# Turning a row of softmax maxima with a VectorE block transpose and eight small transfers per group, where TensorE transposes, a ScalarE eviction and two transfers did it

## The chip, the cores and the metric

The kernel runs on one core of a Trainium2 chip. The metric is the device time of one execution in microseconds (us); lower is better. All times below are in us unless marked ns. The engines are TensorE (PE in the profile, its weight loads PEld), VectorE (DVE), ScalarE (ACT), GpSimd (POOL) and SyncE (SP), which here only issues transfers (DMAs).

## The reference

Two transformer blocks with modulated layer norms act on x of shape (8, 512, 256): attention with 16 heads of width 16, then a feed-forward part. The first block's feed-forward is a gated one with four wide products, the second's is a group of experts. Only attention matters here:

```python
x = L0_attn_x                                    # (8, 512, 256)
h = _layernorm(x) * (1 + ca) + sa
x = x + ga * _L0_attn_ref(h, ...)                # q, k are RMS-normed and rotated
h = _layernorm(x) * (1 + cb) + sb
x = x + gb * _L0_ffn_ref(h, ...)
h = _layernorm(x) * (1 + ca) + sa                # second block, its own ca, sa, ...
x = x + ga * _L1_attn_ref(h, ...)
x = x + gb * _L1_ffn_ref(h, ...)
# inside either attention, for every batch b and head h (T = 512, hd = 16):
scores = jnp.einsum('bhtd,bhsd->bhts', qh, kh) / sqrt(hd)
attn   = softmax(scores, axis=-1)
y      = jnp.einsum('bhts,bhsd->bhtd', attn, vh)
```

## The kernel before

The program is four stages, one after the other: attention of the first block (tiles named A0 in the order below, plain A in the profile; 82 to 600 us of the profiled execution with what precedes its first product), the gated feed-forward (B), attention of the second block (A1 in the order, A in the profile; its first product at 1293.6 us) and the experts (D). The change is in both attention stages.

An attention stage handles 8 batches. The 16 heads of a batch are 4 **groups** of 4 heads; a group is called G and counts from 0 to 31 in a stage. The heads lie in pairs, `a` = 0 and 1, in partitions 0 to 48 and 64 to 112 of the tiles KT (keys) and QS (queries): 48 rows are the high and low parts of 16 features, and row 48 of QS (`QROWS - 1`) holds the negated maximum of each query's scores, so that the product that makes the scores subtracts the maximum as it goes (row 48 of KT is 1).

All engines run one loop over a step p; each writes its own list of instructions for every step, and semaphores alone bind the lists together. In step p:

- TensorE makes two raw products, `SM<-KT,QS` (line 1031; products 2p + 28 and 2p + 29 of the stage, 14 steps ahead of the scores they serve), two score products `ST<-QS,KT` (line 1047), then a **job** if the table has one at p, then `values` (line 1064) in the steps p = 8G + 3, 5, 6, 8. A job is one bank's worth of other work (a projection, transposes); nearly all jobs write the same PSUM bank X, and each waits until the one before it has been evicted.
- VectorE takes the maximum over 512 keys of each raw product, with its sign turned (line 822), 16 for each group, and evicts the jobs P0 and P1 (line 830), both after the step's two maxima.
- ScalarE takes the exponential of 1024 columns of scores (line 584) and evicts most of the other jobs.

SM has two banks, so a raw product waits for the maximum two before it. The maxima of group G are taken in steps 8G - 14 to 8G - 7. They lie as a column for each head and block of 128 queries, one query per partition, and must become a row for each head in QS before step 8G. That is the job MT at step 8G - 5: four transposes of `M` on TensorE into bank X (line 964, a wait for all 16 maxima ahead), an eviction to the tile MT on ScalarE (line 593) at the head of the next step, and at step 8G - 3 on SyncE two transfers of two rows of 1 KB (line 336, columns "A_QS<-A_MT"). TensorE waits for their semaphore `row_ld` before the scores of step 8G.

Other jobs sit at steps that are 1, 2, 4 and 7 mod 8; MT alone is at 3 mod 8, where `values` stand too. In the first block's stage the job before MT is P0 in one group of four (step 18 of each 32) and a projection whose bank ScalarE reads twice (QK, line 610 and `A_sq`, line 613) or once (V) in the others.

SyncE also moves each batch's queries and keys through memory: it loads them back with eight loads of high parts and four of low parts (lines 323 and 329, 128 KB each, called HIGH and LOWS in the tables). Line 1031 waits for all twelve of batch b at step 32b - 14. In the second block's stage the LOWS stand at steps 32b - 21 and 32b - 20, with the store of a finished batch (`y<-A_yT`, line 384) between them.

## Time and profile before

| | us |
|---|---|
| median of 3 runs | 2140.57 |
| lowest and highest of them | 2139.06, 2143.35 |
| the profiled execution, its own time | 2137.07 |
| span of that execution, first to last instruction | 2135.4 |
| TensorE busy | 1860.6 (87%) |
| VectorE busy | 1352.1 (63%) |
| ScalarE busy | 1209.8 (57%) |
| GpSimd busy | 577.1 (27%) |
| attention of the first block, first raw product to last scores | 82.5 to 580.6 |
| attention of the second block, likewise | 1293.6 to 1758.0 |

The span is the time from the first to the last instruction of the profiled execution; 1.7 us of its time lie around it. Busy shares are means over four unlike stages. In a row of the timeline the first number is the start in us from the span's start, the second the duration; what stands in brackets is how long the engine was idle before it and what released it.

### The profile page before, as it was taken

The numbers are of one execution on the slowest core, as the hardware profiler recorded it, in microseconds if no ns is written. First come the engines' busy times: TensorE is split into PE (matmuls) and PEld (weight loads), VectorE is DVE, ScalarE is ACT, GpSimd is POOL, SyncE is SP. The second block draws the span as 40 slices with busy tenths as digits, with TensorE's granted clock in tenths as the row PEclk, the third lists the DMA queues.
The fourth block names the chain that finished last, engine by engine and source line by source line (L and its number), as shares of the span: only waits on it lengthen the run. The fifth ranks groups of instructions, "written<-read, shape, count | busy, mean of one in ns | idle before, by whom it ended". The sixth has DMA issues, their size and how long they took to land. (4 is left out here: it accounts for less than half of the span.)

```text
span 2135.4 us, 29721 instructions
## 1 busy us (share of the span) xinstructions
PE 1860.6 (87%) x10573; PEld 763.6 (36%) x10573; DVE 1352.1 (63%) x2591; ACT 1209.8 (57%) x1686; POOL 577.1 (27%) x668
## 2 busy tenths in 40 slices
PE   5789999988849999999999987899999883888887
PEld 3323332322214444444444442233333221444443
DVE  5578888888624544544534534888888854676771
ACT  4378887776713433333333323888888773565563
POOL 4666667662200000000001022111111001344343
PEclk8689999999979999999999996999999995899999
DMA  3344544334250000000000021233333305323210
GB/s 110 60 107 100 134 121 124 106 106 112 95 217 1 21 21 1 22 21 1 22 18 28 21 50 45 55 69 62 70 61 60 60 11 177 105 101 131 85 40 20
DMA packets 111987, 147.92 MB, mean 69 GB/s; under 512 B 11875, under 2 KB 95189, under 8 KB 109781
## 3 DMA queue, kind: packets, MB, share of 16 engines
q1 hardware_dynamic: 111828, 145.77, 25.6%
q8 instruction: 104, 1.70, 0.4%
q14 instruction: 55, 0.44, 0.1%
HBM read 100.34 MB, written 45.14 MB: 68 GB/s over the span
## 5 line engine op out<-in xcount | busy, mean ns | idle before, releaser
L822 DVE TENSOR_REDUCE A_M<-A_SM 128x1 f16<-128x512 f32 x1024 | 654.4, 687 | 176.4 <-PE A_SM L1031 174.6
L584 ACT ACTIVATE A_P<-A_ST 128x1024 f32<-128x1024 f32 x512 | 523.9, 1026 | 128.6 <-PE A_ST L1047 124.3
L1031 PE MATMUL A_SM<-A_KT,A_QS 48*128 48x512 f16 x1024 | 351.3, 399 | 62.1 <-DVE A_M L822 54.0
L1573 PE MATMUL B_PA<-B_Hh,B_wh 128*128 128x512 f16 x1024 | 388.1, 379 | 0.0
L1573 PE MATMUL B_PA<-B_Hl,B_wh 128*128 128x512 f16 x1024 | 388.1, 379 | 0.0
L1491 ACT ACTIVATE B_af<-B_PA,B_sv 128x512 f32<-128x512 f32 x192 | 132.0, 688 | 367.0 <-PE B_PA L1573 366.9
L1047 PE MATMUL A_ST<-A_QS,A_KT 49*128 49x512 f16 x1024 | 299.9, 386 | 0.3
L1064 PE MATMUL A_AV<-A_P,A_V 128*32 128x512 f32 x2048 | 278.6, 608 | 5.3 <-ACT A_P L584 4.8
L1031 PEld LDWEIGHTS A_SM<-A_KT,A_QS 48*128 48x128 f16 x1024 | 82.4, 93 | 439.5 <-DVE A_M L822 385.2
L1535 DVE TENSOR_SCALAR B_Hh<-B_af 128x512 f16<-128x512 f32 x128 | 58.4, 456 | 281.3 <-ACT B_af L1491 281.3
L1289 POOL TENSOR_TENSOR B_hl<-B_hf,B_hh 128x512 f16<-128x512 f32 x14 | 16.2, 1155 | 543.0 <-ACT B_hh L1305 543.0
L1573 PEld LDWEIGHTS B_PA<-B_Hl,B_wh 128*128 128x128 f16 x1024 | 100.2, 98 | 118.9
L1573 PEld LDWEIGHTS B_PA<-B_Hh,B_wh 128*128 128x128 f16 x1024 | 100.2, 98 | 118.7
L1537 DVE SCALAR_TENSOR_TENSOR B_Hl<-B_af,B_Hh 128x512 f16<-128x512 f32 x128 | 88.6, 693 | 4.4
L1529 DVE SCALAR_TENSOR_TENSOR B_uf<-B_PD,B_sv,B_af 128x512 f32<-128x512 f32 x64 | 47.8, 747 | 54.0 <-PE B_PD L1573 29.6
L550 POOL TENSOR_TENSOR A_tr<-A_qkf,A_tr 128x512 f16<-128x512 f32 x28 | 32.4, 1157 | 156.7 <-ACT A_tr L678 156.7
L1491 ACT ACT_TABLE_LOAD x23 | 29.5, 1283 | 65.6 <-PE B_PA L1573 52.8
L1064 PEld LDWEIGHTS A_AV<-A_P,A_V 128*32 128x32 f32 x2048 | 44.4, 108 | 62.2 <-issue 50.0
L1573 PE MATMUL B_PA<-B_hh,B_wh 128*128 128x512 f16 x128 | 51.0, 399 | 17.0 <-issue 16.9
L934 PE MATMUL A_X<-A_wh,A_hh 128*128 128x256 f16 (+1 forms) x160 | 52.5, 328 | 9.9 <-ACT A_V L628 7.4
L1047 PEld LDWEIGHTS A_ST<-A_QS,A_KT 49*128 49x128 f16 x1024 | 55.5, 94 | 14.4 <-ACT A_P L584 12.3
L2054 DVE SCALAR_TENSOR_TENSOR D_Hl<-D_af,D_Hh 128x512 f16<-128x512 f32 x64 | 45.3, 744 | 16.9 <-ACT D_Hh L1922 16.9
(334 smaller groups left out, 3287.6 us busy)
## 6 DMA issues: line engine op xcount, KB each, us to landing
D_w_st<-in_we_dram SPq DMA_DIRECT2D x16, 1024.0 KB, 4.9
qk<-A_tr SPq DMA_DIRECT2D x58, 256.0 KB, 2.5
A_KT<-qk SPq DMA_DIRECT2D x96, 128.0 KB, 4.7
A_QS<-qk SPq DMA_DIRECT2D x96, 128.0 KB, 5.2
A_w_st<-in_w_ffn_dram SPq DMA_DIRECT2D x32, 352.0 KB, 3.6
w_hi<-A_f_hi SPq DMA_DIRECT2D x32, 176.0 KB, 3.4
w_lo<-A_f_lo SPq DMA_DIRECT2D x32, 176.0 KB, 3.8
B_wl<-w_lo SPq DMA_DIRECT2D x1, 5632.0 KB, 22.5
```

The costliest lines, as they stand in the source:

```text
L584: nc.scalar.activation(P[:, st, 2 * pair:2 * pair + 2, :], ST[:, u % 2, :, :], ACT.Exp, scale=1.0 / math.sqrt(HD)).then_inc(exp_s, 1)
L822: nc.vector.tensor_reduce(M[G % 2][:, tt, o:o + 1], SM[:, n % 2, :], AX, ALU.max, negate=True).then_inc(max_s, 1)
L934: ins = nc.tensor.matmul(out, a, c, start=first and n_ == 0, stop=last and n_ == len(todo) - 1)
L1031: nc.tensor.matmul(SM[:, n % 2, :], QS[b % 2][r, 2 * g + pair, tt * 128:tt * 128 + 128], KT[b % 2][r, 2 * g + pair, :], start=True, stop=T ...
L1047: ins = nc.tensor.matmul(ST[:, u % 2, a, :], KT[b % 2][r, pair, o:o + 128], QS[b % 2][r, pair, :], start=True, stop=True)
L1064: ins = nc.tensor.matmul(AV[32 * j:32 * j + 32, :], V[b % 3][:, st, g * HG + j, :], P[:, st, j, :], start=st == 0, stop=st == TT - 1)
L1491: nc.scalar.activation(af[:, s % 3, :], PA[:, s % 4, :], ACT.Silu if s < HM else ACT.Gelu, scale=sv[:, which, m:m + 1]).then_inc(a_out, 1)
L1529: nc.vector.scalar_tensor_tensor(out=uf[:, s % 2, :], in0=PD[:, s % 2, :], scalar=sv[:, 1, s:s + 1], in1=src, op0=ALU.mult, op1=ALU.mult). ...
L1535: nc.vector.tensor_scalar(Hh[w][:, m, :], src, HS, None, ALU.mult).then_inc(high, 1)
L1537: nc.vector.scalar_tensor_tensor(out=Hl[w][:, m, :], in0=src, scalar=HS, in1=Hh[w][:, m, :], op0=ALU.mult, op1=ALU.subtract).then_inc(spli ...
L1573: ins = nc.tensor.matmul(out, a, c, start=start and kt == 0 and n_ == 0, stop=stop and kt == kts[-1] and n_ == len(ops) - 1)
L2054: nc.vector.scalar_tensor_tensor(out=Hl[:, s, :], in0=af[:, s % 4, :], scalar=HS, in1=Hh[:, s, :], op0=ALU.mult, op1=ALU.subtract).then_in ...
```

## The change

The maxima of a group go into one tile of 128 x 32 (`M`, 16 of its columns used, the rest zeroed once by GpSimd) instead of 128 x 4 x 4. The job MT, its four transposes and its eviction are gone. VectorE turns the tile in blocks of 32 x 32 (`turn_maxima`) at step 8G - 6, between that step's two maxima. In the result, block i of 32 partitions holds the 16 columns as rows, for the queries 32i to 32i + 31 of each block of 128. SyncE, at step 8G - 5, then issues eight transfers (two values of `a`, four of i), each from 8 partitions of 64 bytes to eight pieces of 64 bytes of one row of QS. TensorE's wait before step 8G counts eight transfers (128) where it counted two (32).

```diff
-    jobs |= {8 * G - 5: ("MT", G) for G in range(B * NG)}
...
             def step(p):
-                G = group_at(p, -3)
+                G = group_at(p, -5)
                 if G is not None:
-                    sp.wait_ge(*out("MT", G))
+                    sp.wait_ge(row_s, G + 1)
+                    g, k = G % NG, (G // NG) % 2
                     for a in range(2):
-                        sp.dma_start(QS[(G // NG) % 2][BLK * a + QROWS - 1:BLK * a + QROWS, 2 * (G % NG):2 * (G % NG) + 2, :],
-                                     MTs[G % 2][2 * a:2 * a + 2, :]).then_inc(row_ld[G % 2], 16)
+                        row = QS[k][BLK * a + QROWS - 1:BLK * a + QROWS, 2 * g:2 * g + 2, :].rearrange("o p (t x) -> o (p t) x", t=TT)
+                        for i in range(4):
+                            sp.dma_start(row[:, :, 32 * i:32 * i + 32], rows[G % 2][32 * i + 8 * a:32 * i + 8 * a + 8, :]
+                                         ).then_inc(row_ld[G % 2], 16)
...
+                if p == (slots_of("HL", 0)[1] + 1 if L0 else BEGIN):
+                    for k in range(2):
+                        nc.gpsimd.memset(M[k][:, :], 0.0).then_inc(m_init, 1)
...
-                if name == "MT":
-                    act.wait_ge(*done(name, n))
-                    if n >= 2:
-                        act.wait_ge(row_ld[n % 2], 32 * (n // 2))
-                    nc.scalar.activation(MTs[n % 2][:, :], X16[0:HG, 0:T], ACT.Copy).then_inc(out(name, n)[0], 1)
...
                 if t == 0 and G >= 2:
-                    dve.wait_ge(*done("MT", G - 2))
+                    dve.wait_ge(row_s, G - 1)
+                if t == 0 and G < 2:
+                    dve.wait_ge(m_init, G + 1)
                 dve.wait_ge(raw_mm, n + 1)
-                o = 2 * a + pair
-                nc.vector.tensor_reduce(M[G % 2][:, tt, o:o + 1], SM[:, n % 2, :], AX, ALU.max, negate=True).then_inc(max_s, 1)
+                o = 8 * a + TT * pair + tt
+                nc.vector.tensor_reduce(M[G % 2][:, o:o + 1], SM[:, n % 2, :], AX, ALU.max, negate=True).then_inc(max_s, 1)
+
+            def turn_maxima(G):
+
+                dve.wait_ge(max_s, 16 * (G + 1))
+                if G >= 2:
+                    dve.wait_ge(row_ld[G % 2], 128 * (G // 2))
+                nc.vector.transpose(rows[G % 2][:, :], M[G % 2][:, :]).then_inc(row_s, 1)
...
                 maximum(2 * p + AHEAD)
+                G = group_at(p, -6)
+                if G is not None:
+                    turn_maxima(G)
                 maximum(2 * p + AHEAD + 1)
...
-                if name == "MT":
-                    pe.wait_ge(max_s, 16 * (n + 1))
-                    for tt in range(TT):
-                        ins = nc.tensor.transpose(X16[0:HG, tt * 128:tt * 128 + 128], M[n % 2][:, tt, :], id16[:, :])
...
                 if u == 0 and a == 1:
-                    pe.wait_ge(row_ld[G % 2], 32 * (G // 2 + 1))
+                    pe.wait_ge(row_ld[G % 2], 128 * (G // 2 + 1))
...
-        M = [sb(f"M{k}", [128, TT, HG], F16) for k in range(2)]
-        MTs = [sb(f"MT{k}", [HG, T], F16) for k in range(2)]
+        M, rows = ([sb(f"{n}{k}", [128, 32], F16) for k in range(2)] for n in ("M", "rows"))
```

TensorE's list before, in the first block's stage at steps 18 to 20 of a batch (job P0 at 18, MT at 19, P1 at 20; P0 and P1 are the products of `yTh`, `yTl` with `wp_h`, `wp_l`):

```order
L934 MATMUL A0_X<-A0_yTh,A0_wp_l 128x512
L1031 MATMUL A0_SM<-A0_KT0,A0_QS0 128x512
L1047 MATMUL A0_ST<-A0_QS1,A0_KT1 128x512 x2
L1031 MATMUL A0_SM<-A0_KT0,A0_QS0 128x512
L964 MATMUL A0_X<-id16,A0_M1 4x128 x4
L1064 MATMUL A0_AV<-A0_P,A0_V0 32x512 x4
L1031 MATMUL A0_SM<-A0_KT0,A0_QS0 128x512
L1047 MATMUL A0_ST<-A0_QS1,A0_KT1 128x512 x2
L1031 MATMUL A0_SM<-A0_KT0,A0_QS0 128x512
L934 MATMUL A0_X<-A0_yTh,A0_wp_h 128x512
```

After the change the row of line 964 is gone, and nothing else in that list moves: the values of step 19 follow directly on the raw products, and P1 is the next job on bank X after P0.

VectorE's list after the change, at the same steps (line numbers are the changed kernel's: 821 is the maximum, 836 the eviction of P0 and P1, 828 the new transpose):

```order
L854 RECIPROCAL A0_rden<-A0_AV 128x16
L860 TENSOR_TENSOR A0_yn<-A0_AV,A0_rden 128x4x64
L821 TENSOR_REDUCE A0_M0<-A0_SM 128x1
L828 STREAM_TRANSPOSE A0_rows1<-A0_M1 128x32
L821 TENSOR_REDUCE A0_M0<-A0_SM 128x1 x3
L836 SCALAR_TENSOR_TENSOR A0_xT0<-A0_X,mod,A0_xT0 128x512
```

The transpose stands behind the first maximum of the next group (tile M0) and the two instructions that normalise a finished group; before, the four maxima stood in one piece there.

SyncE's list before, in the second block's stage at steps -27 to -13 of a batch (line 323 the high parts, 329 the LOWS, 336 the row of maxima):

```order
L323 DMA A1_QS0<-qk 16x8x512
L329 DMA A1_KT0<-qk 16x8x512
L329 DMA A1_QS0<-qk 16x8x512
L384 DMA y<-A1_yT 128x2x512
L329 DMA A1_KT0<-qk 16x8x512
L329 DMA A1_QS0<-qk 16x8x512
L336 DMA A1_QS1<-A1_MT0 1x2x512 x2
```

and after the change (322, 328, 386 and 338 are the same four lines):

```order
L322 DMA A1_QS0<-qk 16x8x512
L338 DMA A1_QS1<-A1_rows0 1x8x32 x8
L328 DMA A1_KT0<-qk 16x8x512
L328 DMA A1_QS0<-qk 16x8x512
L386 DMA y<-A1_yT 128x2x512
L328 DMA A1_KT0<-qk 16x8x512
L328 DMA A1_QS0<-qk 16x8x512
L338 DMA A1_QS1<-A1_rows1 1x8x32 x8
```

The row's transfers, now eight, have moved ahead of all four LOWS and of the store.

## Rows read from the trace of the kernel before

**Rows 1.** Attention stages: length, busy PE, PEld, DVE, ACT, POOL; clock, DMA share, GB/s

```profile
82.50:580.60 498.10, 443.57 (x2991) 143.14 (x2990) 415.44 (x734) 371.83 (x502) 286.60 (x344) 0.96 0.42 107
1293.60:1758.00 464.40, 419.98 (x2768) 132.22 (x2768) 360.53 (x658) 371.51 (x490) 68.71 (x93) 0.96 0.28 56
```

**Rows 2.** Costliest group of VectorE: busy, mean ns of one, idle before, releaser

```profile
L822 DVE TENSOR_REDUCE A_M<-A_SM 128x1 f16<-128x512 f32 x1024 | 654.4, 687 | 176.4 <-PE A_SM L1031 174.6
```

**Rows 3.** The removed work, same view

```profile
L593 ACT ACTIVATE A_MT<-A_X 4x512 f16<-4x512 f16 x64 | 36.6, 572 | 5.8 <-PE A_X L964 5.8
L964 PE MATMUL A_X<-id,A_M 128*4 128x128 f16 x256 | 25.2, 222 | 22.6 <-DVE A_xT L830 11.5 <-ACT A_sq L613 5.4 <-ACT A_qkf L621 2.9
```

**Rows 4.** Timeline of TensorE, second block's stage, a step with values, no job

```profile
1505.70 0.39 PE L1031 MATMUL A_SM<-A_KT,A_QS 48*128 48x512 f16 x1
...
1507.25 0.39 PE L1031 MATMUL A_SM<-A_KT,A_QS 48*128 48x512 f16 x1
```

**Rows 5.** Timeline of TensorE, same stage, a step with MT

```profile
1514.49 0.39 PE L1031 MATMUL A_SM<-A_KT,A_QS 48*128 48x512 f16 x1
...
1516.42 0.39 PE L1031 MATMUL A_SM<-A_KT,A_QS 48*128 48x512 f16 x1
```

**Rows 6.** Timeline, first block's stage, step 19 of a batch: MT behind P0

```profile
330.45 0.39 PE L1031 MATMUL A_SM<-A_KT,A_QS 48*128 48x512 f16 x1
...
332.08 0.74 DVE L830 SCALAR_TENSOR_TENSOR A_xT<-A_X,mod,A_xT 128x512 f32<-128x512 f32 x1
...
332.88 0.33 PE L964 MATMUL A_X<-id,A_M 128*4 128x128 f16 x3 [1.82 <-DVE A_xT L830]
...
334.05 0.39 PE L1031 MATMUL A_SM<-A_KT,A_QS 48*128 48x512 f16 x1
```

**Rows 7.** Waits of the transposes of line 964: us, times (PE and PEld)

```profile
  DVE A_xT L830: 26.1, 14
  ACT A_sq L613: 15.2, 24
```

**Rows 8.** Timeline of VectorE, second block's stage: maxima and idle before

```profile
1506.12 1.29 DVE L822 TENSOR_REDUCE A_M<-A_SM 128x1 f16<-128x512 f32 x2 [0.24 <-PE A_SM L1031]
...
1512.98 1.27 DVE L822 TENSOR_REDUCE A_M<-A_SM 128x1 f16<-128x512 f32 x2
...
...
1516.84 1.29 DVE L822 TENSOR_REDUCE A_M<-A_SM 128x1 f16<-128x512 f32 x2 [0.64 <-PE A_SM L1031]
```

**Rows 9.** Who waited for the eviction of line 593

```profile
  PEld A_X L934: 15.5, 30
```

**Rows 10.** The smallest VectorE instructions, and one on 16 columns

```profile
L872 DVE MEMSET A_fence<- 128x1 f32 x16 | 0.9, 59 | 0.0
L848 DVE RECIPROCAL A_rden<-A_AV 128x16 f32<-128x16 f32 x64 | 16.2, 253 | 13.5 <-PE A_AV L1104 13.4
```

**Rows 11.** Issue of the two row transfers: ns, min, median, max

```profile
L336 SPq DMA_DIRECT2D A_QS<-A_MT x128: 558/564/752, 100.8 to 1746.5; - x128
```

**Rows 12.** Transfers by line: KB each, median us from issue to landing

```profile
A_QS<-qk SPq DMA_DIRECT2D x96, 128.0 KB, 5.2
A_b<-A_QS SPq DMA_DIRECT2D x1, 0.5 KB, 1.6
D_row<-D_rowl SPq DMA_DIRECT2D x1, 1.0 KB, 8.5
```

**Rows 13.** Timeline, scores of step 8G: two groups, second block's stage

```profile
1522.22 0.39 PE L1031 MATMUL A_SM<-A_KT,A_QS 48*128 48x512 f16 x1
...
1526.68 2.48 DVE L822 TENSOR_REDUCE A_M<-A_SM 128x1 f16<-128x512 f32 x4
...
1535.71 0.39 PE L1031 MATMUL A_SM<-A_KT,A_QS 48*128 48x512 f16 x1 [0.57 <-DVE A_M L822]
```

**Rows 14.** Timeline, last LOWS of a batch, and its first raw product

```profile
1513.45 0.83 SPq L329 DMA_DIRECT2D A_QS<-qk  x1
...
1525.94 0.39 PE L1031 MATMUL A_SM<-A_KT,A_QS 48*128 48x512 f16 x1
```

More of the change, by code:

```diff
@@ L165, in attention @@
     jobs = {slots_of(name, n)[0]: (name, n) for name in names for n in range(B)}
-    jobs |= {8 * G - 5: ("MT", G) for G in range(B * NG)}
-    assert len(jobs) == B * len(names) + B * NG
+    assert len(jobs) == B * len(names)
     shared = [job for p, job in sorted(jobs.items()) if job not in own]
@@ L218, in attention @@
         job_done, job_out = sem("job_done"), sem("job_out")
+        m_init, row_s = sem("m_init"), sem("row")
         early_done, early_out, turned_done, turned_out = (sem(n) for n in ("early_done", "early_out", "turned_done", "turned_out"))
@@ L246, in attention @@
         banks = {"X": X[:, :]}
-        X16 = X[:, :].bitcast(F16)
         first, later = {}, {}
@@ L587, in out_of_bank @@
             def out_of_bank(name, n):
-                if name == "MT":
-                    act.wait_ge(*done(name, n))
-                    if n >= 2:
-                        act.wait_ge(row_ld[n % 2], 32 * (n // 2))
-                    nc.scalar.activation(MTs[n % 2][:, :], X16[0:HG, 0:T], ACT.Copy).then_inc(out(name, n)[0], 1)
-                elif name in ("T0", "T1"):
+                if name in ("T0", "T1"):
                     f = int(name[1])
@@ L642, in step @@
                 if name[:2] == "QK" or name[0:1] == "V":
-                    out_of_bank(name, n)
-                name, n = jobs.get(p - 1, ("", 0))
-                if name == "MT":
                     out_of_bank(name, n)
@@ L960, in job @@
                     pe.wait_ge(ones_s, 1)
-                if name == "MT":
-                    pe.wait_ge(max_s, 16 * (n + 1))
-                    for tt in range(TT):
-                        ins = nc.tensor.transpose(X16[0:HG, tt * 128:tt * 128 + 128], M[n % 2][:, tt, :], id16[:, :])
-                elif name in ("T0", "T1"):
+                if name in ("T0", "T1"):
                     f = int(name[1])
```

## The prediction

> **What bounds the kernel now.** I read first how busy each engine is within the two attention stages, since the change touches nothing else [rows 1]. In the first block's stage TensorE is busy for 444 of 498 us, VectorE for 415; in the second's TensorE for 420 of 464, ScalarE for 372, VectorE for 361. No engine is full. TensorE leads in both; VectorE is close behind in the first. Then I read the costliest group of VectorE [rows 2]: ahead of the maxima it idles 176 us, nearly all of it waiting for a raw product. So VectorE waits for TensorE's list, not the reverse. What one step of that list takes is read from the timeline, raw product to raw product. A step with values and no job takes 1507.25 - 1505.70 = 1.55 us [rows 4]; a step with values and MT takes 1516.42 - 1514.49 = 1.93 us [rows 5]. In the first block's stage, where MT stands behind P0, it takes 334.05 - 330.45 = 3.60 us [rows 6]: the transposes need bank X, the bank is freed by VectorE's eviction, and that stands behind two maxima in VectorE's list.
>
> **The change, part by part.** The sum is made against the profiled execution, 2137.07 us.
>
> *1. TensorE's step without MT.* 64 steps, of three kinds.
> - Second block, 32 steps: 1.93 - 1.55 = 0.38 us each, 12 us.
> - First block behind P0, 8 steps: 3.60 - 1.55 = 2.05 us. Part of it comes back. The eviction of P0 ends at 332.82 [rows 6] and P1 now needs it. In step 19 TensorE was through with the four products ahead of the job at 332.88 - 1.82 = 331.06, 0.6 us into the step; it would come to P1 at 330.45 + 1.55 + 0.6 = 332.6 and wait 0.2. Net 1.85 us, times 8 is 15 us.
> - First block, the other 24: here MT waits for ScalarE, which reads the bank of the job before it. Behind a QK job these waits are 15.2 us, 24 times [rows 7]; weight load and product of one stall both count, so it is some 0.6 us in each of 12 steps, and behind V, whose bank is read once, less. I take 0.4 us of wait per step and 0.3 us for the transposes themselves (a little under the 0.38 of the second block, which has some wait in it). 0.7 times 24 is 17 us.
>
> On TensorE that is 44 us. Another way to it: 0.3 x 64 and the 22.6 us for which the products of line 964 were held up [rows 3] make 42. Bounds: from below 0.38 x 64 = 24; from above the QK stalls uncut, 15.2/12 + 0.3 = 1.57 us in all 24 steps, 65.
>
> *2. What VectorE lets through.* VectorE's own work does not shrink, so the time can fall only as far as its idle time does. In the first block's stage that is 498 - 415 = 83 us [rows 1]. Where it lies: the maxima after a normal step wait 0.24 us, those after MT's step 0.64 [rows 8]. The second value falls to the first: 0.4 us, as in 1, so the second block's 12 us pass through. In the first block 32 us would have to come out of 83, and VectorE would go from 83% busy to 89%. It has work queued (line 830, statistics, copies of turned heads) behind which part of TensorE's stall is hidden already. I let three quarters through, 24 us; bounds 8 (a quarter) and 32. Together 36 us.
>
> *3. The eviction on ScalarE goes.* 64 x 0.572 = 36.6 us of busy time [rows 3]. It counts only where somebody waited for it: the next job's weight loads, 15.5 us over 30 waits [rows 9]. In part of each the array was still finishing earlier products, and some of those steps have slack on the other engines. I take 6 us; bounds 0 and 15.5.
>
> *4. The transpose on VectorE.* 64 of them. The trace has none. The nearest rows are a memset at 59 ns and an operation on 16 columns at 253 ns [rows 10]. I take 0.12 us for 32 columns of 2 bytes, nearer the small instruction since it reads no PSUM: 7.7 us in all, bounds 3.8 and 16. Its waits are met already (the 16th maximum is two instructions back). The cover is VectorE's wait for raw products, 0.24 us before the maxima of a normal step [rows 8]; it is mostly there in the second block and partly in the first. 3 us on the path. If the cover were gone it would be 8.
>
> *5. The row's transfers.* They must land before the scores of step 8G. The trigger is now the transpose in step 8G - 6. In the group at 1512.98 the first maximum of that step ends at 1512.98 + 0.64 [rows 8], the transpose 0.1 later, near 1513.7; scores are due at 1522.22 [rows 13], a lead of 8.5 us. In the next group it is 1535.71 - (1526.68 + 0.62 + 0.12) = 8.3 [rows 13]. The lead shrinks by the 0.4 us that MT's step loses: 7.9. Needed: eight issues. Issues of line 336 take 0.56 us each [rows 11]; with the gap between two I take 0.59, so the last begins 7 x 0.59 = 4.1 us after the first. A small transfer within SBUF landed 1.6 us after issue [rows 12]. 4.1 + 1.6 = 5.7 us, 2.2 before they are due. Cost 0. If the cover is gone: each 0.1 us more per issue uses 0.7 of the 2.2. A transfer with loads ahead of it landed after 8.5 us [rows 12]: then this group's scores would be late by some 4.7.
>
> The Trainium skill speaks against this trade ("DMA: Bandwidth & Descriptors", "Rules for kernel authors": join many small transfers into one, since under 64 KB one pays mostly overhead; "Anatomy of one DMA" gives some 2.0 us fixed for each). Overlapped, its figure would put the last landing at 4.1 + 2.0 = 6.1 us, an estimate, and the cost stays 0; one after the other it is 16 us, far over the lead. That the two transfers' semaphore is never what ends a wait of TensorE, here VectorE is [rows 13], fits overlapped.
>
> *6. What is queued behind them on SyncE.* Eight issues hold SyncE for 4.7 us, 3.5 more than two. At most steps it waits long ahead of time. The place that counts is the second block's step 32b - 21, where the LOWS now stand behind the row. The row is issued from 1513.7 to 1518.4, then four LOWS and a store, 2.6 us; the last begins at about 1520.2 instead of 1513.45 [rows 14]. With the median landing of 5.2 us [rows 12] it is there at 1525.4; the raw product that needs it came at 1525.94 [rows 14], now some 0.4 earlier. That is a tie. If landing takes 3 us longer behind the store, TensorE waits 3 us. Six batches have this pattern: 0 to 18 us, I take 3. What is late next then are the maxima, at once.
>
> **Sum.** -36 - 6 + 3 + 0 + 3 = -36 us: 2101.1 for the profiled execution. The median of the runs shown is 3.5 us above that execution, so 2104.6; I say **2105 us**.
>
> **The rivals.** A measurement of this kernel can tell about 0.2%, 4 us, from no change.
>
> *A. The forecast holds, 0.66.* Its own range is 2092 to 2120: the 44 us of part 1 with hardly anything held back, or half of them with the costs of 4 and 6.
>
> *B. The stall moves to VectorE, 0.17.* For it: 415 of 498 us busy in the first block, and evictions and statistics bunched in the same steps. Then the first block gives only 8 us, the second 8, the eviction nothing, and the transposes cost their full 8 in both stages: -8 us, or -16 if they are covered: 2125 to 2133. Against it: before the maxima that follow MT's step VectorE waits visibly [rows 8].
>
> *C. More comes back, 0.07.* The full 44 us of TensorE and 12 of part 3, less 3: 2088.
>
> *D. The rows come late, 0.09; slower.* Place: TensorE's wait before step 8G. Price: if an issue with eight scattered pieces takes t, the last lands at 7t + 1.6, against 7.9. It bites from t = 0.9 us, and eats the whole gain where 7t + 1.6 - 7.9 exceeds 36/64 = 0.56 us, at t = 0.98. At t = 1.2 it is 2.1 us in each of 64 groups, 134 us, less the 36: 2239. For it: the long landing of `D_row`. Against: the 128 issues of today hardly differ, 558 ns the least and 564 the median [rows 11]. By the skill's figure taken one after the other (same page as above) this is the case that would come.
>
> *E. Nothing measurable, 0.01 beside the edges of B.*
>
> **How the numbers follow.** Likeliest A: 2105. To leave out no more than 2 in 10, the range takes A whole, C's value and most of B, and leaves out D (0.09) and tails of B and C: 2088 to 2130. Faster by over 0.2%: A, C and nearly all of B, 0.88. Within 0.2%: 0.03. Slower: D, 0.09.
>
> **What the profile of the changed kernel would show.** Part 1: raw product to raw product in steps 3 mod 8 at 1.55 to 1.6 us, and 2 us less at step 19 of the first block; the maxima wait less than 176 us in all, by about 30. Part 3: no wait of a job's weight load on a 4x512 eviction. Part 4: 64 transposes at 0.06 to 0.25 us. Part 5: 512 issues at about 0.56 us, and no wait of line 1047 on `A_QS<-A_rows`; such a wait, 64 times, is D. Part 6: a wait of line 1031 on `A_QS<-qk` or `A_KT<-qk` in the second block, up to six times. B would show as VectorE above 90% busy in the first block's stage with the stage hardly shorter. The forecast would be most wrong if the eight transfers cost more each than the two did.

## The result: 0.44% slower, and the profile after

The changed kernel takes 2149.74 us (median of 14 runs, 2144.16 to 2159.4); the kernel before, beside it on the same chip, 2140.25 us (14 runs, 2137.23 to 2151.03). The ratio is 1.0044, 95% interval 1.0028 to 1.0061: some 9 us slower, where I had forecast 36 us faster. The profiled execution of the changed kernel took 2146.28 us, span 2144.6; numbers by stage, step and wait are of the profiled executions, ratios of all.

First the busy time by stretch of the changed kernel, cut as [rows 1]: attention of the first block, the feed-forward stage, attention of the second block. Columns as there.

```profile
85.90:579.60 493.70, 445.78 (x2865) 140.31 (x2864) 418.77 (x766) 356.54 (x470) 287.15 (x344) 0.93 0.44 108
579.60:1297.60 718.00, 659.84 (x3101) 307.67 (x3097) 311.71 (x635) 236.66 (x332) 43.44 (x49) 0.96 0.11 34
1297.60:1767.70 470.10, 421.84 (x2640) 128.97 (x2640) 364.57 (x690) 357.92 (x458) 68.98 (x95) 0.93 0.27 55
```

Against [rows 1] the first stage is 4.4 us shorter and the second block's 5.7 longer. TensorE does 126 and 128 products fewer and is yet 2 us *longer* busy in each: the column of its clock reads 0.93 for 0.96, and a raw product that takes 0.39 us takes 0.61 at half clock. The feed-forward stage, where nothing changed, went from 713.0 us to 718.0; its row before, for comparison:

```profile
580.60:1293.60 713.00, 657.00 (x3101) 307.80 (x3097) 311.01 (x635) 236.12 (x332) 43.39 (x49) 0.97 0.11 34
```

The stretch ahead of the first attention took 85.9 us for 82.5; it takes either of the two in kernels of both kinds (85.7 in the kernel before with one line moved, 82.1 in the changed one with one line moved), so it is not the change's. Of the 9.2 us between the two profiled executions the two attention stages, which alone were changed, hold only 1.3; 5.0 lie in the feed-forward stage and 3.4 in the stretch ahead. Against a forecast of -36 us the attention stages missed by 37.

Then TensorE's step where MT stood behind P0, which is [rows 6] in the changed kernel (timeline):

```profile
330.92 0.68 DVE L821 TENSOR_REDUCE A_M<-A_SM 128x1 f16<-128x512 f32 x1
331.52 0.20 DVE L828 STREAM_TRANSPOSE A_rows<-A_M 128x32 f16<-128x32 f16 x1
...
332.58 0.39 PE L1036 MATMUL A_SM<-A_KT,A_QS 48*128 48x512 f16 x1
...
334.11 0.39 PE L1036 MATMUL A_SM<-A_KT,A_QS 48*128 48x512 f16 x1
```

The step takes 334.11 - 332.58 = 1.53 us for 3.60. The stall is gone, as forecast. Step 3 of a second-block batch went from 2.02 us (1499.48 to 1501.50 before) to 1.54 (1503.34 to 1504.88). Step 19 of such a batch, which also had an MT, went only from 2.09 to 2.00. So most of what was taken out came out, and something gave it back. The list of waits names new ones (us, times, longest):

```profile
POOL A_f_hi L437 <- DMA A_w_st<-in_w_ffn_dram: 36.4, 6, 10.5
DVE A_f_max L895 <- POOL A_f_lo L439: 15.8, 7, 4.4
PEld A_SM L1036 <- DMA A_QS<-qk: 7.8, 6, 1.8
PE A_SM L1036 <- DMA A_QS<-qk: 6.4, 6, 1.6
DVE A_tr L845 <- DMA qk<-A_tr: 5.3, 4, 2.5
DVE A_st L872 <- DMA A_xt<-x_tok: 2.7, 1, 2.7
PE A_ST L1052 <- DMA A_QS<-A_rows: 2.3, 1, 2.3
```

Before, the first was 9.1 us in 2 times, the second 4.8 in 2, the fifth 2.6 once, and the third, fourth and the last two were not there. The first, GpSimd's wait for weights, stands only from 400 us on, in the first block's last four batches, and still holds 23.2 us in the fastest run but one (`bounce_seen`, below); the others matter. Where they stand is seen in VectorE's groups in the first block's stage. Before (82.5 to 580.6 us), then after (85.9 to 579.6):

```profile
L822 DVE TENSOR_REDUCE A_M<-A_SM 128x1 f16<-128x512 f32 x512 | 326.6, 686 | 81.0 <-PE A_SM L1031 79.6
L889 DVE TENSOR_REDUCE A_f_max<-A_f_lo 128x1 f32<-128x704 f16 x31 | 27.2, 878 | 1.2 <-POOL A_f_lo L437 1.2
L839 DVE COPY A_tr<-A_X 128x1024 f16<-128x1024 f16 x28 | 19.2, 685 | 2.9 <-DMA qk<-A_tr 2.6 <-PE A_X L1003 0.3
```

```profile
L821 DVE TENSOR_REDUCE A_M<-A_SM 128x1 f16<-128x512 f32 x512 | 327.5, 683 | 63.0 <-PE A_SM L1036 61.7
L895 DVE TENSOR_REDUCE A_f_max<-A_f_lo 128x1 f32<-128x704 f16 x31 | 27.2, 878 | 11.5 <-POOL A_f_lo L439 11.4
L845 DVE COPY A_tr<-A_X 128x1024 f16<-128x1024 f16 x28 | 19.2, 684 | 5.9 <-DMA qk<-A_tr 5.3 <-PE A_X L1008 0.5
...
L828 DVE STREAM_TRANSPOSE A_rows<-A_M 128x32 f16<-128x32 f16 x32 | 6.5, 202 | 0.0
```

The maxima wait 18 us less. Of these 10.3 went to waits for GpSimd, 3.0 to waits for a transfer and 6.5 to the transposes. Together that is 19.8 us, more than what came free. Two smaller waits of VectorE fell by 2.5, and its instructions overlap at their ends, so these columns do not add up to the stage's 4.4; they show where freed time went.

The new wait for GpSimd, once in full. VectorE reduces a part of the feed-forward weights (`f_max`, line 895, step 23 of a batch) that GpSimd has split (lines 437 and 439). Timelines of the changed kernel, VectorE, TensorE, GpSimd:

```profile
277.00 1.28 DVE L821 TENSOR_REDUCE A_M<-A_SM 128x1 f16<-128x512 f32 x2
280.38 0.89 DVE L895 TENSOR_REDUCE A_f_max<-A_f_lo 128x1 f32<-128x704 f16 x1 [2.10 <-POOL A_f_lo L439]
281.18 1.28 DVE L821 TENSOR_REDUCE A_M<-A_SM 128x1 f16<-128x512 f32 x2
```

```profile
278.65 0.62 PE L1008 MATMUL A_X<-id,A_qkh 128*128 128x128 f16 x8
281.92 0.61 PE L1036 MATMUL A_SM<-A_KT,A_QS 48*128 48x512 f16 x1 [2.65 <-DVE A_M L821]
```

```profile
274.63 2.27 POOL L508 TENSOR_TENSOR A_hl<-A_hf,A_hh 128x512 f16<-128x512 f32 x2
276.86 1.16 POOL L498 TENSOR_TENSOR A_qkl<-A_qo,A_qkh 128x512 f16<-128x512 f32 x1
277.97 0.77 POOL L437 CAST A_f_hi<-A_w_st 128x704 f16<-128x704 f32 x1
278.82 1.52 POOL L439 TENSOR_TENSOR A_f_lo<-A_w_st,A_f_hi 128x704 f16<-128x704 f32 x1
```

GpSimd works without a pause from 257.5 us to the end of this piece at 280.3. In the same batch before, it ended this piece at 276.44 + 1.53 = 277.97 and VectorE's reduction began at 278.39, without a wait: TensorE's stalls at MT had kept VectorE just behind GpSimd. With them gone VectorE comes first and hands the wait to its maxima, and TensorE stands 2.65 us. Its products then take 0.61 us for 0.39: half clock, from 280.7 to 287.5.

To find where a stage gives time back I took the length of each batch (32 steps) from the start of step 0's first raw product to the next such, last batch to its last scores, in us:

```
first block   b0    b1    b2    b3    b4    b5    b6    b7
before        64.2  61.1  61.1  61.1  62.6  58.4  55.1  47.5
after         63.0  61.2  61.7  61.0  57.7  59.0  55.6  47.7
second block
before        59.2  55.4  55.4  55.4  55.4  55.4  53.7  43.9
after         62.6  54.4  54.5  54.5  55.0  54.1  56.8  49.3
```

In batches 1 to 3 of the first block steps 3, 11, 19 and 27 become 4.2 us shorter, and step 23 (+2.2) with steps 24, 25 and 0 takes it back. In batches 1 to 5 of the second block the same steps become 1.5 us shorter, 1.8 with the steps behind them, and step 17 takes 0.7 to 1.6.

The first and the last two batches of the second block lose more, 3.4, 3.1 and 5.4 us, and this is most of that stage's loss. In the first of them a load of x stands behind the eight issues on SyncE, at step 15; VectorE waits for it, and TensorE for VectorE (timelines of SyncE, VectorE, TensorE):

```profile
1349.53 5.41 SPq L338 DMA_DIRECT2D A_QS<-A_rows  x8
1354.99 0.44 SPq L343 DMA_DIRECT2D A_xt<-x_tok  x1
```

```profile
1358.92 0.43 DVE L872 BATCH_NORM_STATS2 A_st<-A_xt 128x6 f32<-128x256 f32 x1 [2.67 <-DMA A_xt<-x_tok]
```

```profile
1360.00 0.60 PE L1036 MATMUL A_SM<-A_KT,A_QS 48*128 48x512 f16 x1 [2.72 <-DVE A_M L821]
```

At the end of this stall the clock is halved, from 1359.3 to 1366.1 us, and steps 15 to 17 take 4.8 us more than before. Likewise from 1693.8 to 1704.0, behind a wait of 1.3 us for `A_QS<-qk`: steps 19 to 22 of batch 6 then take 3.2 us more, with no new wait among them. And from 1724.5 to 1731.3 (2.3 us more) and from 1758.6 to 1765.5, behind a wait of 2.3 us for the row. Before, the second block had no half clock after 1336.4 us. The stretches as windows (the last three numbers are clock, DMA share, GB/s):

```profile
1359.30:1366.10 6.80, 6.10 (x26) 2.34 (x28) 4.51 (x10) 3.94 (x5) 1.16 (x1) 0.50 0.00 0
1693.80:1704.00 10.20, 9.22 (x42) 1.33 (x40) 6.65 (x11) 4.98 (x5) 0.00 (x0) 0.50 0.01 0
```

### The profile page after: what moved, and what is told of

It reads as the page before. It is cut to its first block and busy times, and to the rows that moved or that the text cites. A ratio compares the mean times of both kernels' runs of the same rounds, so it can differ in the third digit from the quotient of the medians.

```text
span 2144.6 us, 29537 instructions
## 1 busy us (share of the span) xinstructions
PE 1870.8 (87%) x10317; PEld 760.1 (35%) x10317; DVE 1359.7 (63%) x2655; ACT 1181.6 (55%) x1622; POOL 578.3 (27%) x672
## 5 line engine op out<-in xcount | busy, mean ns | idle before, releaser
L1036 PE MATMUL A_SM<-A_KT,A_QS 48*128 48x512 f16 x1024 | 358.5, 406 | 81.5 <-DVE A_M L821 67.1
L1052 PE MATMUL A_ST<-A_QS,A_KT 49*128 49x512 f16 x1024 | 309.1, 397 | 2.3 <-DMA A_QS<-A_rows 2.3
L1069 PE MATMUL A_AV<-A_P,A_V 128*32 128x512 f32 x2048 | 286.1, 632 | 5.7 <-ACT A_P L589 3.8
L508 POOL TENSOR_TENSOR A_hl<-A_hf,A_hh 128x512 f16<-128x512 f32 x30 | 34.5, 1159 | 85.4 <-ACT A_hh L659 85.4
```

Source lines behind the costliest of these rows:

```text
L1036: nc.tensor.matmul(SM[:, n % 2, :], QS[b % 2][r, 2 * g + pair, tt * 128:tt * 128 + 128], KT[b % 2][r, 2 * g + pair, :], start=True, stop=T ...
L1052: ins = nc.tensor.matmul(ST[:, u % 2, a, :], KT[b % 2][r, pair, o:o + 128], QS[b % 2][r, pair, :], start=True, stop=True)
L1069: ins = nc.tensor.matmul(AV[32 * j:32 * j + 32, :], V[b % 3][:, st, g * HG + j, :], P[:, st, j, :], start=st == 0, stop=st == TT - 1)
```

## The experiments

Ratios are to the kernel before, run beside them. "Clock" is the granted clock, mean over the runs of a kernel: before 0.9416, after 0.9261.

### GpSimd's lead

**The reduction two steps later** (`seen_late`), and the same edit in the kernel before (`before_seen`).

```diff
-                    if p - 3 in STAGE_AT:
-                        i = STAGE_AT.index(p - 3)
+                    if p - 5 in STAGE_AT:
+                        i = STAGE_AT.index(p - 5)
```

> The changed kernel with one edit: VectorE's reduction of a weight part (line 895) stands five steps behind GpSimd's part instead of three. Theory 1 (the stall moved to GpSimd's chain: with MT gone TensorE and VectorE reach step 23 of a batch 2 us earlier and VectorE then waits for GpSimd's part): the waits of line 895, 15.8 us now, fall to under 3, step 23 of the first block's batches falls from 4.1 to about 2.3 us, and the kernel gets 8 to 15 us faster than the changed one: 2136 to 2142, ratio to before 0.998 to 1.001. Theory 2 (SyncE's eight issues delay the loads that GpSimd needs, so GpSimd is late whatever VectorE waits for): under 4 us. Theory 3 (clock: TensorE's half-speed stretches carry the loss): no change beyond 3 us, unless the stretches fall as well.

Measured 1.0031 (1.0011 to 1.005). The wait for GpSimd went from 15.8 us to 5.1, but batches 1 to 3 took 60.6, 61.6 and 60.9. The list of waits shows where it went:

```profile
DVE A_tr L845 <- DMA qk<-A_tr: 8.3, 4, 2.8
PEld A_SM L1036 <- DMA A_QS<-qk: 8.3, 6, 1.7
```

VectorE's next stop is the copy of turned heads in step 0, whose buffer a store must have left that stands behind the eight issues on SyncE. Two resources run late here, not one. The gain, 3 us by the ratios, is within their intervals; 8 to 15 had been expected.

> The kernel before with its weight part's reduction five steps behind instead of three: a control. Theory: before, the maxima's stalls of TensorE let GpSimd finish in time (4.8 us of waits), so the edit is worth 0 to 3 us: ratio 0.998 to 1.001. Rival (the reduction's place alone is worth what the two edits gained together): 2128 to 2134, ratio 0.994 to 0.997.

Measured 0.9985 (0.9968 to 1.0001): the place of the reduction is worth 3 us in the kernel before, which the interval does not tell from nothing.

**GpSimd's work shortened** (`after_gp`, `before_gp`): the low part of the weights is computed for 64 of 704 columns and left zero elsewhere, so the kernel leaves out the low parts of the other columns.

```diff
-                nc.gpsimd.tensor_tensor(f_lo[:, i % 2, :], src, hi, ALU.subtract).then_inc(f_low, 1)
+                nc.gpsimd.tensor_tensor(f_lo[:, i % 2, 0:64], src[:, 0:64], hi[:, 0:64], ALU.subtract).then_inc(f_low, 1)
```

> The changed kernel with the same cut on GpSimd. Theory 1 (in the first block the change only uncovers GpSimd's chain of some 51 us from step 30 to step 25 of the next batch): the batches of the first block fall from 61 to 57 or 58 us, and the kernel is 12 us or more faster than the changed one; the gap to before_gp is -6 to -12 us where it is +9 without the cut. If SyncE or the clock hold the batch, the gap stays above 0.

> The kernel before with GpSimd's subtraction on a weight part cut from 704 to 64 columns (the low part is set to zero once instead; it is zero for these weights): 32 x 1.3 us less on GpSimd in the first block. If GpSimd's chain does not bound the kernel before (theory 1: it is just covered by MT's stalls), it gains under 5 us on before: ratio 0.998 to 1.0. If GpSimd bounds it already, 20 us or more.

Measured: after 1.0003 (0.9985 to 1.002), before 0.9993 (0.998 to 1.0006). The first block's stage fell from 493.7 to 485.4 us in the changed kernel and stayed in the one before (498.3 for 498.1). So GpSimd's lead bounds the changed kernel and not the one before. The changed kernel gained 9 us by the ratios, where 12 or more had been expected. Batches 1 to 3 still took 59.8, 60.2 and 59.3, for 57.8 in `bounce_seen` below, where SyncE has less to issue.

### SyncE's slots

**The last loads of a batch ahead of the row** (`lows_first`; the table of the second block).

```diff
-LOWS=(27, 27, 28, 28)
+LOWS=(26, 26, 26, 26)
```

> The changed kernel with one edit: in the second block the four LOWS of a batch are issued at step 32b - 22, ahead of the row's eight transfers and of the store. Theory 2 (SyncE): step 17 of each batch of the second block, 2.9 us now, goes back to 1.7, six times, and the kernel gets 6 to 9 us faster than the changed one: 2141 to 2144, ratio 1.000 to 1.002. Theory 1 and theory 3: nothing, ratio 1.004.

Measured 1.0022 (1.0004 to 1.004). The wait for `A_QS<-qk` is gone and the one for the row has come:

```profile
PEld A_ST L1052 <- DMA A_QS<-A_rows: 13.1, 7, 2.6
PE A_ST L1052 <- DMA A_QS<-A_rows: 11.1, 7, 2.3
```

**Both edits** (`seen_lows`).

> Both edits. If theories 1 and 2 each hold for their own stage they add up: 15 to 22 us faster than the changed kernel, 2128 to 2135, ratio 0.994 to 0.998. If theory 3 holds alone: 2147 to 2150.

Measured 1.0003 (0.9987 to 1.0019): 9 us under the changed kernel and not the 15 to 22 expected, since TensorE still waits for the row, 7.9 us in 7 times.

**The row last in SyncE's step** (`rows_last`): the loop of eight transfers moved behind the step's stores and loads, and the reduction two steps later.

> The changed kernel with the eight transfers issued last in SyncE's step, behind the stores and loads of that step, and the weight part's reduction five steps behind. Theory (SyncE has no slack for eight issues in any order): the wait for the store behind them at the start of a batch goes, so that batches 1 to 3 of the first block take 58 to 60 us, but rows come late in the second block (waits for the row of 5 to 13 us), ratio 0.997 to 1.002, 2134 to 2146 us. Rival (only the order was bad): both waits go, 2128 to 2133.

Measured 0.9972 (0.9953 to 0.9991). First-block batches 60.6, 57.8, 59.6, 60.5; the wait of the copy is 2.7 us, that for the row 13.8 in 10 times. As with `lows_first`, an order only chooses who waits.

**Two transfers for eight** (`light`): from the ninth group on only one of the four pieces of each row is moved, the other three keep old values; and with the reduction moved too (`light_seen`).

```diff
-                        for i in range(4):
+                        for i in range(4 if G < 8 else 1):
```

> The changed kernel in which, from the ninth group of each stage on, only two of the eight row transfers are issued (a = 0 and 1 for the first block of 32 queries); the other maxima in QS are those of an earlier batch. It leaves out three quarters of the rows' update, and measures what SyncE's load costs. Theory 2: all that SyncE's occupation costs comes back, 15 us or more faster than the changed kernel, in both stages. Theory 1: in the second block step 17 comes back (7 us), in the first block step 23 stays at 4 us, since GpSimd's own work decides it: 6 to 9 us faster, ratio 1.000 to 1.002.

> Two of eight row transfers from the ninth group on (three quarters of the rows' update left out), and VectorE's reduction of a weight part five steps behind instead of three. With two transfers alone it was 2138.2. If what the later reduction freed was lost again to SyncE's late store and loads (in that run step 0 of a batch grew by 2 to 3 us), both edits together give more than either: the first block's batches 0 to 3 fall to 58 or 59 us and the kernel to 2125 to 2132, ratio 0.992 to 0.995. If GpSimd's chain holds the batch whatever VectorE waits for, the batches stay at 61 and the kernel at 2136 to 2139.

Measured: `light` 0.9983 (0.9968 to 0.9999), `light_seen` 0.9931 (0.9911 to 0.995). With two transfers no wait for `A_QS<-qk` is left and second-block batches 2 to 5 take 53.7 us: 1.7 less than before, which is by how much steps 3, 11 and 27 and the steps behind them are shorter. With the reduction moved as well, batches 2 to 4 of the first block fall to 57.8. In both kernels the first eight groups of a stage still have eight transfers, and in both the first batch of the second block still waits some 3 us for x.

**The whole row in three transfers** (`bounce`, `bounce_seen`): one store of the turned 128 x 32 block to memory at step 8G - 5, two loads at step 8G - 4; everything is computed.

```diff
+                    sp.dma_start(d["rowbuf"][G % 2], rows[G % 2][:, :]).then_inc(row_st[G % 2], 16)
+                G = group_at(p, -4)
+                if G is not None:
+                    sp.wait_ge(row_st[G % 2], 16 * (G // 2 + 1))
                     g, k = G % NG, (G // NG) % 2
                     for a in range(2):
-                        for i in range(4):
-                            sp.dma_start(row[:, :, 32 * i:32 * i + 32], rows[G % 2][32 * i + 8 * a:32 * i + 8 * a + 8, :]
+                        sp.dma_start(QS[k][BLK * a + QROWS - 1:BLK * a + QROWS, 2 * g:2 * g + 2, :].rearrange("o p (t i x) -> o (p t) i x", i=4, x=32),
+                                     d["rowbuf"][G % 2].rearrange("(i r) x -> r i x", i=4)[8 * a:8 * a + 8, :, :].unsqueeze(0)).then_inc(row_ld[G % 2], 16)
```

> The row through memory alone (one store, two loads a group), the weight part's reduction where the changed kernel has it, three steps behind. Theory (the eight issues on SyncE cost the second block its late transfers, GpSimd's lead the first block): second block batches near 53.7 us, first block batches 1 to 3 near 61; 2130 to 2138 us, ratio 0.995 to 0.999. Rival (the issues alone were the cause, and the reduction's place does nothing): 2114 to 2122, as with both edits.

> The whole computation, with the row written to memory once (128 x 32) at step 8G-5 and read back with two loads at step 8G-4: three issues a group for eight; the weight part's reduction five steps behind. Theory (SyncE's slots and GpSimd's lead carry the loss): like the run with two transfers and the moved reduction, 2129 to 2135 us, ratio 0.992 to 0.996, batches 2 to 4 of the first block near 57.8 us and those of the second near 53.7. Rival (rows through memory come late): waits for the row of over 5 us in either block, and 2138 to 2150.

Measured: `bounce` 0.9939 (0.9921 to 0.9958), `bounce_seen` 0.9883 (0.9852 to 0.9914). Both are faster than the kernel before, and than I expected. Attention of `bounce_seen`, as windows:

```profile
85.90:565.30 479.40, 442.69 (x2863) 138.25 (x2862) 415.92 (x766) 356.37 (x470) 286.58 (x344) 0.95 0.46 112
...
1285.90:1744.00 458.10, 418.18 (x2638) 128.47 (x2638) 363.81 (x690) 356.49 (x458) 68.85 (x95) 0.95 0.28 57
```

479.4 and 458.1 us stand against 498.1 and 464.4 in [rows 1]. VectorE in the first stage:

```profile
L824 DVE TENSOR_REDUCE A_M<-A_SM 128x1 f16<-128x512 f32 x512 | 327.5, 684 | 63.1 <-PE A_SM L1039 61.8
L898 DVE TENSOR_REDUCE A_f_max<-A_f_lo 128x1 f32<-128x704 f16 x31 | 27.2, 877 | 0.0
L848 DVE COPY A_tr<-A_X 128x1024 f16<-128x1024 f16 x28 | 19.1, 684 | 3.3 <-DMA qk<-A_tr 2.8 <-PE A_X L1011 0.4
```

The maxima wait no more and no less than in the changed kernel; the two other waits are gone or as before. That is the 14 us between 493.7 and 479.4, and it shows both causes at once. Nor does VectorE wait for x any more in the second block's first batch, which takes 57.8 us. By the two ratios the eight issues cost 1.0044 - 0.9939 = 1.05% (22 us), the place of the reduction 0.56% (12 us), with intervals of some 0.25 and 0.35 points on either side. These are the prices of the two in this order; with the eight issues in place, moving the reduction gave 3 us (`seen_late`).

### MT kept, and TensorE's clock

**The change with MT left in** (`both`): the transposes of the maxima and ScalarE's eviction run as before, and nobody reads them.

> The changed kernel with the old job MT kept as idle ballast: TensorE still makes the four transposes at step 8G - 5 and ScalarE still evicts them, but QS is filled by VectorE's transpose and the eight transfers. TensorE's list is then that of the kernel before, SyncE's and VectorE's those of the changed one. If SyncE's eight issues and VectorE's transposes cost what they seem to (late LOWS in six batches, 7 us; transposes 64 x 0.2, partly covered), it is 7 to 15 us slower than before, ratio 1.003 to 1.007, and slower than the changed kernel by little or nothing, since what MT's removal gave in the first block was lost again. If TensorE's half-speed stretches come from the denser list without MT (theory 3), the mean granted clock returns from 0.927 to about 0.94.

Measured 1.0061 (1.0041 to 1.0082), clock 0.9399. So the new parts by themselves cost 0.6%, 13 us. Taking MT out gives back 4 by the ratios, which the intervals do not tell from nothing. In the profiled executions the two attention stages took 504.0 and 475.6 us with MT left in, for 493.7 and 470.1 without: it does give some 16 us there, about what the new parts cost, but the feed-forward stage takes 713.4 us with it and 718.0 without. The clock came back and the kernel is no faster than the changed one; as MT's own cost came back with it, this does not tell what the clock alone is worth.

**One product more** (`fill`), four more (`fill4`), and one more in the kernel before (`before_fill`). The product is the same as the one behind it and writes the same place.

```diff
+                if n % 16 == 2:
+                    nc.tensor.matmul(SM[:, n % 2, :], QS[b % 2][r, 2 * g + pair, tt * 128:tt * 128 + 128],
+                                     KT[b % 2][r, 2 * g + pair, :], start=True, stop=True)
```

> The changed kernel with a second, identical raw product issued every 16th step (step 2 mod 16) ahead of the real one: TensorE has some 0.2 to 0.4 us more work there and no new wait; nothing else changes. Theory that TensorE's half clock follows how it stands idle at the batch boundaries and at the weight part's waits: granted clock stays 0.923 to 0.931 and the time is 2149 to 2158. Rival (the clock came down because TensorE has less work without the maxima's transposes): clock back to 0.936 or more and feed-forward stage back to about 713 us, time 2138 to 2148.

> The changed kernel with four further identical raw products at step 2 mod 16 for one: some 1 us more work on TensorE there, and no wait. Theory (the clock follows TensorE's work in that step): granted clock 0.936 to 0.942, feed-forward stage near 713 us; the products cost up to 0.6 us in each of 64 steps, so 2138 to 2158 us. Rival (the one product's effect on the clock was chance): clock 0.926 to 0.931, 2155 to 2185 us.

> The kernel before with one further identical raw product at step 2 mod 16: a control for the last two. If that product works through the clock, it has little to give back here: clock 0.941 to 0.945, ratio 0.998 to 1.003. Rival (the product helps by itself, whatever the clock): ratio 0.993 to 0.997.

Measured: `fill` 0.9995 (0.9973 to 1.0018), clock 0.9322; `fill4` 1.0175 (1.0157 to 1.0193), 0.9354; `before_fill` 1.0016 (1.0002 to 1.003), 0.9432. The changed kernel, given 64 needless products, gets 0.5% faster; the kernel before gets slower by what they cost. The clock rose each time, so my theory for `fill`, that it follows only how TensorE stands idle, falls. But the clock is not all of what `fill` gained. Its attention stages took 493.2 and 471.6 us, for 493.7 and 470.1, 1.0 more in all; the same product cost the kernel before 5.6 us there (501.0 and 467.1, for 498.1 and 464.4), so some 5 us may have come back with the clock. What `fill` gained outright in the profiled execution lies in the feed-forward stage:

```profile
579.10:1292.20 713.10, 657.32 (x3101) 308.39 (x3097) 310.80 (x635) 236.18 (x332) 43.41 (x50) 0.97 0.11 34
```

That is `fill`: 713 us again, for 718. Yet `fill4` has a higher clock and 721 us, and `bounce_seen` and `bounce_fill` (below) have 720.6 and 713.9. I compared TensorE's gaps in the stage. All kernels have two of 4 to 5 us, near 290 and 455 us into it; those of 717 us and more have further ones near 37, 208, 374 and 540 us, most of 0.9 to 1.6 us, between the same products. Nothing recorded ends them (in the list of waits they count as "issue"). Most of the excess is there. So the 5 us are not the clock's: they come and go with TensorE's list ahead of the stage, the only thing that `fill` changes. The number of products ahead does not decide it alone, since `fill4` has as many in the first block as the kernel before, and 721 us. What TensorE waits for in these gaps stays open.

**All together** (`bounce_fill`): `bounce_seen` and the one product.

> The row through memory, the reduction five steps behind, and the second, identical raw product every 16th step. If the changed kernel's loss is in part a lower clock that more work on TensorE gives back, the granted clock goes from 0.936 to 0.940 or more and the time from 2117 to 2108 to 2114. Rival (chance): clock 0.934 to 0.938, 2115 to 2122.

Measured 0.9867 (0.9846 to 0.9888), 2113.32 us, clock 0.9407. It is the fastest, 28 us under the kernel before; by the intervals it can't be told from `bounce_seen`. The attention stages of the two add up to the same 937.5 us, 25 under the 962.5 of the kernel before: what the products cost there and what the clock gave back cancel.

## Why the prediction was wrong, point by point

Two steps of the sum failed, one for each block. In the first block it is the second term: "VectorE's own work does not shrink, so the time can fall only as far as its idle time does", with "I let three quarters through". I looked for what VectorE waits for, TensorE, and not for what would make it wait once TensorE is earlier: 4.4 us came through for 24. In the second block it is "Cost 0" for the row's transfers, with the 3 us for the last LOWS: I took 12 us to pass through, and the stage grew by 5.7, because SyncE's eight issues held back the transfers behind them and half-clock stretches followed on the waits. A third part, the 5.0 us of the feed-forward stage, no step of the sum could have had; its cause is open.

- *Part 1, TensorE's step without MT: right for one step, too high in the sum.* Step 19 fell by 2.1 us and step 20 took 0.35 back, 1.7 net (I had 2.05, net 1.85); steps 3 and 11 of the first block fell by 0.6 to 0.7, step 27 by 0.9 (0.7), steps 3, 11 and 27 of the second by 0.4 to 0.5 and step 19 by 0.1 (0.38 for all four). In the first block's batches 6 and 7 steps 3 and 11 fell by only 0.1. Over all MT steps, four of them longer now at half clock, it is 24 and 8 us for 32 and 12.
- *Part 2, what VectorE lets through: wrong, and the cause of the first block's miss.* Its idle time ahead of the maxima fell by 18 us in the first block (I had 24 through), but its waits for GpSimd and for a store rose by 13.3. The whole stage became 4.4 us shorter, where this term had 24. "VectorE is close behind" was the wrong neighbour: GpSimd, 287 of 498 us busy in [rows 1], works without a pause for 23 us ahead of this reduction. A busy share over a stage hid a chain with no slack. `after_gp`, `before_gp` and `bounce_seen` show it.
- *Part 3, the eviction:* no weight load waits for it any more; what it brought of the 6 us can't be told apart.
- *Part 4, the VectorE transpose:* 202 ns for 120, 12.9 us in all, inside the bounds. What they cost on the path (I had 3) no run tells apart from the transfers; `both` has all new parts together at 13.
- *Part 5, the row's transfers:* forecast last landing 5.7 us after the first issue and 2.2 in reserve. Measured: eight issues in 5.4 us, landing 1.0 us later, 6.4; in the second block 1.3 to 2.4 us in reserve in most groups. One group was late, the last: near the end TensorE has no raw products left, its steps are shorter and the lead with them, and this row landed 7.0 us after its first issue.

```profile
1757.73 0.39 PE L1052 MATMUL A_ST<-A_QS,A_KT 49*128 49x512 f16 x2 [2.26 <-DMA A_QS<-A_rows]
```

  As far as the row goes this was right. Its cost of 0 was not: I asked only when the row lands, not what SyncE's 5.4 us do to the other transfers, except for part 6. They also held back the load of x at step 15 of the second block's first batch (2.7 us of waiting, 4.8 us in all).
- *Part 6, the last LOWS: right in mechanism, mis-sized.* Forecast six ties and 3 us; there were six waits, 6.4 us, for the second block's step 17. SyncE's queue and the raw product that waited (timeline):

```profile
1517.00 5.41 SPq L338 DMA_DIRECT2D A_QS<-A_rows  x8
1522.46 0.44 SPq L328 DMA_DIRECT2D A_KT<-qk  x1
...
1524.40 0.84 SPq L328 DMA_DIRECT2D A_QS<-qk  x1
```

```profile
1529.79 0.39 PE L1036 MATMUL A_SM<-A_KT,A_QS 48*128 48x512 f16 x1 [0.97 <-DMA A_QS<-qk]
```

  The last load begins 7.4 us after the row's first (I had 6.5) and lands by 1529.8, 5.4 later (I had 5.2).
- *Missing altogether:* the store behind the same issues at step 27 of the first block (`seen_late`), the load of x, and TensorE's clock. In the profiled executions the half-clock time rose from 42 to 68 us in the first attention and from 36 to 62 in the second. Its price I can only estimate, in two ways. In batches 6 and 7 of the second block 10.2 us at half clock went with 3.2 us more time and 6.8 with 2.3; at that price the 52 us more of half clock are 16 to 18 us. And over 277 executions of the 18 kernels, each against its own kernel's mean, 0.001 less clock goes with 1.2 us more time (1.1 within the kernel before); from 0.9416 to 0.9261 that is 17 to 19 us. The second is correlation, and both may count a stall twice, since in the rows above half clock follows on stalls that cost time themselves. `fill` and `bounce_fill` agree in sign: their products cost attention 1.0 and 0.0 us, for 5.6 in the kernel before, while half clock fell by 8 and 20 us there. That half clock costs time is borne out by all of these; how much of the loss is its own is not shown.
- *The rivals.* B (the stall moves to VectorE) had the right engine and the wrong reason, and stopped at 2133. D (rows late) had the sign, for a cause that occurred once. No rival had a third engine's chain, and of SyncE's other transfers part 6 alone had one.
- *The Trainium skill* had been weighed on landing times alone. "DMA: Bandwidth & Descriptors", "Rules for kernel authors", advises joining small transfers; the runs agree: three for eight took 1.0044 to 0.9939. The same page ("Issuing engines are not separate DMA queues") calls the time to initiate a transfer usually small beside the transfer. Here eight issues take 5.4 us and the last lands 1.0 us after them; the measurement decides, and it was the issuing that cost. The fixed 2.0 us that the prediction took from this page ("Anatomy of one DMA") is stated there for transfers issued from GpSimd, and these are SyncE's: from the start of the last issue to the landing it took 1.7 us.

With the eight issues and the reduction's place undone, `bounce_fill` gains 28 us, three quarters of the 36 forecast, 25 of them in the attention stages. The gain was there, behind two queues that had no slack.

## What to carry to other kernels

When a stall is removed, list every engine and queue whose work the stalled one waits for a little later, and look at when each *finishes* there, not at its busy share: a stage average of 58% hid a chain without a pause. A transfer costs its issue as much as its landing: count what is queued behind it on the issuing engine, at every step of the period and at the loop's thin end. And read an unchanged stage too: it moved by 5 us here, over half of the measured difference, without one instruction of it being edited.

## What the runs showed of the hardware that I had not expected

- Small transfers within SBUF on SyncE cost 635 ns of issue each in the median (634 the least, 1569 the most of 512), for 558 to 564 of the two longer ones in [rows 11]; a 128 x 32 block to memory 338 ns:

```profile
L338 SPq DMA_DIRECT2D A_QS<-A_rows x512: 634/635/1569, 99.3 to 1755.4; - x171
```

```profile
L335 SPq DMA_DIRECT2D rowbuf<-A_rows x64: 320/338/644, 99.3 to 1730.3; - x64
```

  So a trip through memory (1.4 us from issue to landing for the store, two loads of 658 ns issue; 1.7 us of issuing for 5.4) was cheaper for SyncE than eight direct pieces.
- VectorE's transpose of 128x32 two-byte elements took 200 to 204 ns, 64 times; I had taken 120.
- The granted clock fell from 0.942 to 0.926 with the change. With the 256 short products back it was 0.940 (`both`); with 64 needless ones 0.932 (`fill`), and 0.941 for 0.936 on top of `bounce_seen`. Of the nine half-clock stretches that are new in the changed kernel's attention, seven began at or just behind an idle time of TensorE of 1.3 to 2.7 us, two (523.0 and 1724.5 us) behind one of 0.8.
- The feed-forward stage took either 713 to 714 us or 717 to 721 with the same instructions, depending on a few gaps of TensorE of about 1 us that no recorded wait ends.
